# Graph network layer on one core: three buffers for gathered rows instead of five, a gather queue one turn ahead, and the statistics of the early rows moved into the turns

## The reference, cut to what matters

```python
h = relu(layernorm(x))                       # 6250 nodes x 128, float32
W = silu(edge_attr @ fw1 + fb1) @ fw2 + fb2  # 206250 edges x 50 -> x 128, the filters
t = silu(h @ aw1 + ab1) @ aw2 + ab2          # the node table
msg = W * t[src]                             # one gathered row of t for each edge
agg = segment_sum(msg, dst)                  # dst is sorted
return x + h + silu(agg @ ow1 + ob1) @ ow2 + ob2
```

## Time and profile before

| | |
|---|---|
| median of three runs | 2394.53 us (2394.49 to 2397.1) |
| the profiled execution | 2395.59 us |
| its span, first to last instruction | 2393.7 us |
| POOL busy | 1525.4 us, 64% |
| PE busy | 1300.2 us, 54% |
| DVE busy | 1178.2 us, 49% |
| ACT busy | 520.4 us, 22% |
| mean granted clock of PE | 0.74 |

### The profile page before, as it was taken

The page is one execution under the profiler, slowest core; times in us unless marked ns, Lnnn a source line. Parts: engine busy times, 40 slices in busy tenths (PEclk is TensorE's granted clock), DMA queues, the critical chain, the costliest instruction groups (busy, mean ns, idle before and its releaser), DMA issues.

```text
span 2393.7 us, 13107 instructions
## 1 busy us (share of the span) xinstructions
PE 1300.2 (54%) x4526; PEld 701.8 (29%) x4526; DVE 1178.2 (49%) x1404; ACT 520.4 (22%) x545; POOL 1525.4 (64%) x1619
## 2 busy tenths in 40 slices
PE   2425665656554655566556555655655454555545
PEld 1313332323332333233223222323332232232323
DVE  3635454545554554555535544644454453554545
ACT  2312222212221222222222211211222121121211
POOL 7246666666666666666666666666666666666664
PEclk8667776778777677777668777876778686776776
DMA  4312122212212222212212212212212212212211
GB/s 140 143 30 79 45 80 81 75 54 84 82 51 81 53 75 79 81 47 82 86 45 83 80 46 88 79 50 84 83 51 80 81 50 81 80 51 85 56 46 37
DMA packets 62292, 171.46 MB, mean 72 GB/s; under 512 B 27088, under 2 KB 29648, under 8 KB 59024
## 3 DMA queue, kind: packets, MB, share of 16 engines
q0 software_dynamic: 51584, 105.75, 17.1%
q1 hardware_dynamic: 8192, 61.32, 6.8%
q10 hardware_dynamic: 2448, 3.54, 0.4%
HBM read 164.08 MB, written 6.42 MB: 71 GB/s over the span
## 4 chain that ended last, share of the span: by engine, by line
another core or an unknown queue 40%; PE 27%; ACT 15%; issue 14%; DVE 3%; DMA 0%; ACTq 0%; SPq 0%; DVEq 0%
PE banks L872 15%; ACT hid L435 7%; PE banks L864 7%; ACT hid L441 7%; PE banks L879 3%; PE banks L887 1%; PE banks L811 1%; ACT hs L455 1%; DVE stats L643 0%; ACT mid L464 0%; DVE stats L544 0%; PE banks L806 0%; PE banks L818 0%; DMA xs<-in_x 0%
## 5 line engine op out<-in xcount | busy, mean ns | idle before, releaser
L369 POOL DMA_INDIRECT xg<-node_table,src x1564 | 1478.6, 945 | 828.3 <-issue 453.2
L872 PE MATMUL banks<-hid,wts 128*128 128x512 f32 x806 | 535.3, 799 | 565.4 <-ACT hid L435 436.6
L672 DVE TENSOR_TENSOR banks<-banks,xg 128x1024 f32<-128x1024 f32 (+1 forms) x198 | 241.0, 1217 | 1090.2 <-remote 899.2
L864 PE MATMUL banks<-attr,wts 50*128 50x512 f32 x806 | 293.9, 810 | 444.8 <-issue 250.4
L675 DVE TENSOR_REDUCE sums<-banks 128x128 f32<-128x1024 f32 (+1 forms) x408 | 493.9, 1211 | 13.6
L441 ACT ACTIVATE hid<-banks,cols 128x1024 f32<-128x1024 f32 x202 | 224.5, 1111 | 914.0 <-remote 425.7
L435 ACT ACTIVATE hid<-banks,cols 128x1024 f32<-128x1024 f32 x202 | 224.4, 1111 | 825.0 <-remote 595.9
L872 PEld LDWEIGHTS banks<-hid,wts 128*128 128x128 f32 x806 | 179.9, 248 | 755.3 <-ACT hid L435 467.6
L879 PEld LDWEIGHTS banks<-ident,hid 128*128 128x128 f32 x1612 | 225.5, 171 | 204.2 <-issue 198.2
L879 PE MATMUL banks<-ident,hid 128*128 128x128 f32 x1612 | 284.5, 333 | 0.0
L679 DVE TENSOR_TENSOR banks<-banks,other 128x1024 f32<-128x1024 f32 (+1 forms) x204 | 248.7, 1219 | 7.0
(11 more groups left out here) (89 smaller groups left out, 279.5 us busy)
## 6 DMA issues: line engine op xcount, KB each, us to landing
attr<-in_attr SPq DMA_DIRECT2D x25, 2048.0 KB
xg<-node_table,src POOLq DMA_INDIRECT x1564, 2.5
out<-res ACTq DMA_DIRECT2D x8, 256.0 KB
xs<-in_x SPq DMA_DIRECT2D x3, 512.0 KB, 6.0
node_table<-res SPq DMA_DIRECT2D x3, 512.0 KB, 2.8
out<-res ACTq DMA_DIRECT2D x5, 192.0 KB
spare<-in_dst SPq DMA_DIRECT2D x1, 808.0 KB
src<-in_src SPq DMA_DIRECT2D x1, 808.0 KB
```

What stands on the lines that cost most here:

```text
L369: pool.indirect_dma_start(xg[:, i % XG, j, :], None, table[:, :], bass.IndirectOffsetOnAxis(ap=src[:, s * L + j:s * L + j + 1], axis=0))\
L672: dve.tensor_tensor(to, to, rows_of, ALU.mult).then_inc(signal, 1)
L864: i = pe.matmul(hid_ps[:, GC * half:GC * half + GC], fw1_s[at, :], attr[at, cols_of], start=True, stop=True)
L872: i = pe.matmul(hid_ps[:, at], w["fw2_s"][:, :], hid[:, s % 2, at], start=True, stop=True)
```

## The change

- `XG` is 3 instead of 5, and `REACH = XG - LAG = 1`: POOL starts the gathers of turn s when the filters of turn s - 1 are done. Only the first three turns have no wait.
- The 48 early gathers are no longer issued in one go: those for the third to the sixth early turn wait for points of the node chunks (the transposes of chunk 0, the result of chunks 0, 1 and 3).
- The statistics of the early tiles are taken by DVE within turns 1 to 6 (8 `bn_stats` each), the moments in turn 7 and the scales in turn 9; ACT's square root comes in turn 8, between its silu activations. The first early task starts in turn 10 (before, in turn 0), and the early turns are 30, 50, 72, 92, 114, 136 instead of 20, 40, 64, 84, 108, 128.
- The one-hots are made for one turn at a time, with one `tensor_scalar` and one `scalar_tensor_tensor` of 128x88, in place of three operations of 128x176 every second turn. There are six buffers of one turn instead of three of two.
- The three parts of `fb2` are made only in the fallback loop.
- At the end ACT does the activation of the last output task ahead of the store of the one before it.

```diff
@@ -16,7 +16,7 @@
 PAIR_EDGES = L * P
 PAIRS = -(-N_EDGES // PAIR_EDGES)
 EDGE_TILES = PAIRS * L
-XG = 5
+XG = 3
 SETS = 4
 PART = 8
 EARLY_PAIRS = 6
@@ -34,8 +34,7 @@
 R_WINDOWS = 14
 RW = 453
 AGG = R_WINDOWS * RW
-BATCH = 2
-OH_SETS = 3
+OH_SETS = 6
 assert AGG >= STEP * (PAIRS - 1) + WIN and AGG >= LEAD + NODE_TILES * P
@@ -46,7 +45,7 @@
 assert len(GROUP_OF) == PAIRS and all(STEP * (n - 1) + WIN <= 512 for _, n in GROUPS)
-EARLY_TURNS = (20, 40, 64, 84, 108, 128)
+EARLY_TURNS = (30, 50, 72, 92, 114, 136)
 MAIN_TURNS = [s for s in range(PAIRS) if s not in EARLY_TURNS]
 MAIN_OF = {s: i for i, s in enumerate(MAIN_TURNS)}
 EARLY_OF = {s: i for i, s in enumerate(EARLY_TURNS)}
@@ -70,6 +69,8 @@
 for s in range(HALVED[0]):
     SUMS_AT.setdefault(s + LAG + (s in OPENS), []).append(s)
 assert SETS > LAG + 1
+
+REACH = XG - LAG
@@ -95,6 +96,12 @@
+STAT_TURNS = tuple(range(1, EARLY_PAIRS + 1))
+VAR_TURN, STD_TURN, SCALE_TURN, EARLY_FROM = 7, 8, 9, 10
+assert VAR_TURN > STAT_TURNS[-1]
+
+
+
 EARLY_STEPS = dict(relu=0, transposed=1, copied=2, first=3, middle=4, second=5, rows=6)
 OUT_STEPS = dict(first=0, middle=1, second=2, rows=3, stored=4)
@@ -106,7 +113,7 @@
 def tasks():
-    done, free, outs, halves = [], 0, list(range(len(OUTS) - 1)), list(range(2 * EARLY_PAIRS))
+    done, free, outs, halves = [], EARLY_FROM, list(range(len(OUTS) - 1)), list(range(2 * EARLY_PAIRS))
     for s in range(PAIRS):
         if s < free:
             continue
@@ -227,7 +234,7 @@
         xg = sb("xg", [P, XG, L, F])
         hid = sb("hid", [P, 2, PC])
         sums = sb("sums", [P, SETS + 2, 2, F])
-        onehot = sb("onehot", [P, OH_SETS, BATCH, 2, WIN])
+        onehot = sb("onehot", [P, OH_SETS, 2, WIN])
         e_x = sb("e_x", [P, EARLY_PAIRS * L, F])
@@ -353,7 +360,12 @@
             pool.wait_ge(s_pool, 3)
             pool.wait_ge(e_src_in, 16)
+
+            table_at = {2: (s_tr, 0), 3: (s_res, 0), 4: (s_res, 1), 5: (s_res, 3)}
             for t in range(EARLY_PAIRS * L):
+                if t % L == 0 and t // L in table_at:
+                    signal, c = table_at[t // L]
+                    pool.wait_ge(signal, run(c))
                 pool.indirect_dma_start(e_x[:, t, :], None, x[:, :],
                                         bass.IndirectOffsetOnAxis(ap=e_src[:, t:t + 1], axis=0)).then_inc(e_gathered[t // L], 16)
             pool.wait_ge(src_in, 16)
@@ -363,7 +375,7 @@
                 if i >= XG:
-                    pool.wait_ge(fil_done, run(s - 2))
+                    pool.wait_ge(fil_done, run(s - REACH))
                 for j in range(tiles_in(s)):
                     landed = half_gathered[2 * HALVED.index(s) + 2 * j // tiles_in(s)] if s in HALVED else gathered[i % XG]
                     pool.indirect_dma_start(xg[:, i % XG, j, :], None, table[:, :],
@@ -425,9 +437,6 @@
             act.wait_ge(s_cover, 4)
             act.activation(other[:, :], same, ACT.Identity, bias=ones[:, 0:1], scale=-1.0).then_inc(s_other, 1)
-            act.wait_ge(s_var, 3)
-            act.activation(e_moments[:, 2, :], e_moments[:, 2, :], ACT.Sqrt).then_inc(s_std, 1)
-
             def silu_hid(s):
                 n = tiles_in(s) * P
@@ -445,11 +454,16 @@
                     if a < PAIRS:
                         silu_hid(a)
                         add_fb2(a)
+                if s == STD_TURN:
+                    act.wait_ge(s_var, 3)
+                    act.activation(e_moments[:, 2, :], e_moments[:, 2, :], ACT.Sqrt).then_inc(s_std, 1)
             def task(kind, step, b, n):
                 if step == "relu":
                     if n >= 2:
                         act.wait_ge(n_tr, n - 1)
+                    if n == 0:
+                        act.wait_ge(s_rstd, 3)
                     for j in range(TPG):
                         t = n * TPG + j
                         i = act.activation(hs[:, n % 2, j, :], e_x[:, t, :], ACT.Relu, bias=e_moments[:, 3, t:t + 1],
@@ -471,12 +485,11 @@
             act.wait_ge(s_hx, run(N_CHUNKS - 1))
             act.wait_ge(s_left, 1)
-            act.wait_ge(s_rstd, 3)
             turns(pair, task)
+            task("out", "middle", len(TASKS), len(OUTS) - 1)
             for left in STEPS.get(PAIRS, ()):
                 task(*left)
-            for step in ("middle", "stored"):
-                task("out", step, len(TASKS), len(OUTS) - 1)
+            task("out", "stored", len(TASKS), len(OUTS) - 1)
             n = edges_left(act)
             for i in range(2):
                 act.wait_ge(s_out[i], 16 * len(OUTS[i::2]))
@@ -595,21 +608,6 @@
             i.then_inc(s_cover, 1)
             dve.tensor_tensor(low, first_ps, d_last.rearrange(flat), ALU.min).then_inc(s_cover, 1)
             dve.tensor_tensor(high, first_ps, d_last.rearrange(flat), ALU.max).then_inc(s_cover, 1)
-
-            dve.tensor_copy(fb2_part[:, 0, :], rows[:, 0, :]).then_inc(s_fb2, 1)
-            dve.wait_ge(s_fb2, 1)
-            dve.tensor_tensor(fb2_rest[:, 0, :], rows[:, 0, :], fb2_part[:, 0, :], ALU.subtract).then_inc(s_fb2, 1)
-            dve.wait_ge(s_fb2, 2)
-            dve.tensor_copy(fb2_part[:, 1, :], fb2_rest[:, 0, :]).then_inc(s_fb2, 1)
-            dve.wait_ge(s_fb2, 3)
-            dve.tensor_tensor(fb2_rest[:, 1, :], fb2_rest[:, 0, :], fb2_part[:, 1, :], ALU.subtract).then_inc(s_fb2, 1)
-            dve.wait_ge(s_fb2, 4)
-            dve.tensor_copy(fb2_part[:, 2, :], fb2_rest[:, 1, :]).then_inc(s_fb2, 1)
-            dve.wait_ge(s_fb2, 5)
-            dve.wait_ge(s_set, 1)
-            for i in range(3):
-                dve.tensor_copy(fb2_rows[32 * i:32 * i + 1, :, :],
-                                fb2_part[32 * i:32 * i + 1, i:i + 1, :].to_broadcast([1, TPG, F])).then_inc(s_fb2, 1)
             dve.tensor_tensor(ends[:, 0, :], first_ps, bases[:, :], ALU.subtract).then_inc(s_rel, 1)
             dve.tensor_tensor(ends[:, 1, :], last_ps, bases[:, :], ALU.subtract).then_inc(s_rel, 1)
@@ -637,15 +635,13 @@
             dve.tensor_scalar(n_left[:, :], left_ps, -1.0, float((EDGE_TILES + PAIRS) * P), ALU.mult,
                               ALU.add).then_inc(s_left, 1)
-            for t in range(EARLY_PAIRS * L):
-                if t % L == 0:
-                    dve.wait_ge(e_gathered[t // L], 16 * L)
-                i = dve.bn_stats(stats[:, t, :], e_x[:, t, :])
-            i.then_inc(s_step, 1)
-            step[0] += 1
-            dve.wait_ge(s_step, step[0])
-            moments_of(stats[:, 0:EARLY_PAIRS * L, :], e_moments)
-            scales_of(e_moments, 3)
+            def early_stats(r):
+                dve.wait_ge(e_gathered[r], 16 * L)
+                for t in range(r * L, (r + 1) * L):
+                    i = dve.bn_stats(stats[:, t, :], e_x[:, t, :])
+                if r == EARLY_PAIRS - 1:
+                    i.then_inc(s_step, 1)
+                    step[0] += 1
             dve.wait_ge(s_hx, run(N_CHUNKS - 1))
             dve.wait_ge(s_pool, 3)
@@ -654,15 +650,12 @@
             dve.wait_ge(s_tab, 16 * (AHEAD + table_writes(N_CHUNKS - 1)))
-            def one_hots(k):
-                first, n = k * BATCH, min(BATCH, PAIRS - k * BATCH)
-                nodes = iota[:, 0:WIN].rearrange("p (o w) -> p o w", o=1).to_broadcast([P, n, WIN])
-                for m in range(2):
-                    of_row = ends[:, m, first:first + n].rearrange("p (n o) -> p n o", o=1).to_broadcast([P, n, WIN])
-                    dve.tensor_tensor(onehot[:, k % OH_SETS, 0:n, m, :], nodes, of_row, ALU.is_equal).then_inc(oh_done, 1)
-                dve.wait_ge(oh_done, 3 * k + 2)
-                dve.tensor_tensor(onehot[:, k % OH_SETS, 0:n, 1, :], onehot[:, k % OH_SETS, 0:n, 1, :], onehot[:, k % OH_SETS, 0:n, 0, :],
-                                  ALU.subtract).then_inc(oh_done, 1)
+            def one_hots(s):
+                nodes, to = iota[:, 0:WIN], onehot[:, s % OH_SETS, :, :]
+                dve.tensor_scalar(to[:, 0, :], nodes, ends[:, 0, s:s + 1], None, ALU.is_equal).then_inc(oh_done, 1)
+                dve.wait_ge(oh_done, 2 * s + 1)
+                dve.scalar_tensor_tensor(out=to[:, 1, :], in0=nodes, scalar=ends[:, 1, s:s + 1], in1=to[:, 0, :],
+                                         op0=ALU.is_equal, op1=ALU.subtract).then_inc(oh_done, 1)
             def by_tile(s, h, n):
@@ -687,8 +680,7 @@
             def pair(s):
-                if s % BATCH == 0:
-                    one_hots(s // BATCH)
+                one_hots(s)
                 if s in HALVED:
                     by_halves(s)
                     return
@@ -711,6 +703,13 @@
                 mask(msg, s * L, L, masked)
                 dve.wait_ge(masked, run(s))
                 row_sums(s % SETS, 1, msg).then_inc(red_done, 1)
+                if s in STAT_TURNS:
+                    early_stats(STAT_TURNS.index(s))
+                elif s == VAR_TURN:
+                    dve.wait_ge(s_step, step[0])
+                    moments_of(stats[:, 0:EARLY_PAIRS * L, :], e_moments)
```

(20 more changed lines are left out.)

## The result

The kernel took 2356.81 us in the median of four runs (2353.55 to 2362.83), against 2394.51 for the one before beside it. The ratio is 0.9846, with a 95% interval of 0.9822 to 0.9869: 37.7 us off, where I had forecast 17.5. The profiled execution took 2358.69 us, with a span of 2356.9.

The account below looks back on a forecast made before the run. The prediction took PE's signals, arriving late when POOL has issued gathers for long, to bound the kernel. Terms -20 + 2 + 3 + 3 - 6 = -18 gave a span of 2375.7, hence 2377 us, range 2332 to 2436.

Parts of the forecast that it names:

- places and reach: Steady turns: no price; the loop through DVE's sums asks 6.2 us a turn, hidden under POOL's 10.0.
- +2 (statistics): Turns 1 to 6: 1.9 us of DVE statistics in each, of which the first flush may show one, +2 us.
- +3 (root): Early turns: the root takes ACT out of its silu tables and back, +3 us, between 0 and 18.
- +3 (one-hots): All turns: the new one-hot operations touch POOL's gathers, taken as +3 us; DVE's own time 0.
- The start: Up to turn 5's gathers: first main gather at 90, turn 3 at 140, turn 5 at about 164, -20 us.
- this wait goes: Start: PE's hidden no longer waits until ACT has the root at 155.78; part of the start's -20 us.
- The end: After the last gathers begin: the last multiply follows about 8 us later, before 15.4; -6 us (0 to -9).
- A stop each turn: Rival, steady turns: filters arrive over 10.0 us after the last, so every turn stops; +300, 2677 us, chance 0.08.
- Long stretches go: Rival, steady turns: POOL's three-turn stretches break into twos, some 16 more stops of 3.4; +55, 2432 us, chance 0.20.
- The compare locks POOL: Rival, one-hots: the new tensor_scalar compare holds up POOL's gathers, +34 instead of +3; 2408 us, chance 0.05.
- Start gains nothing: Rival, start: held signals move from the early gathers to the first 24 main ones; +20, 2397 us, chance 0.10.
- Sooner signals: Rival: stops come after less running, half are 2 us shorter, the start gains more; -40 more, 2337 us, chance 0.12.

## Why the prediction was too small

**What bounds the kernel: right, with a limit that I didn't see.** Late signals bound it, and they went on doing so as forecast (waits after the first 305.6 us, forecast 305). I took them for a property of kernel and chip. They are a condition that comes and goes, and a saving that consists of shorter late signals goes with it. And I laid them on PE, while DVE's own steps come late as well. In the loop of places and reach four operations of 1.23 are 4.9 us and not 5.1, which changes nothing.

**The step that failed is the middle,** the terms +2 (statistics), +3 (root), +3 (one-hots), and no price for places and reach. It measured -3.4 instead of +8: 11.4 of the missing 18.9 us; the start and the end, each sized too small, make the other 4.7 and 2.8. None of the three +'s shows in POOL's times. All the 48 statistics are done by 188, behind the sums of turns 1 to 6, at 9.8 us against 11.2 with 11.9 of gaps before. The root with its two loads of tables:

```profile
201.64 1.28 ACT L459 ACT_TABLE_LOAD   x1
202.94 0.24 ACT L459 ACTIVATE e_moments<-e_moments 128x48 f32<-128x48 f32 x1
203.20 1.28 ACT L444 ACT_TABLE_LOAD   x1
...
213.34 1.11 ACT L450 ACTIVATE hid<-banks,cols 128x1024 f32<-128x1024 f32 x1 [7.73 <-issue]
```

It takes ACT 2.8 us. PE's `hidden` for the next silu ended at 202.81, so that silu comes some 1.6 us later than it could. Behind it PE ends the filters' product at 209.34 and ACT takes it at 213.34, 4.0 us late, so the 1.6 were probably swallowed. The kernel with all of this ahead of the turns isn't fit to price it with late signals: its middle of 2186.0 is of another batch, and its ratio, 0.9837, differs from 0.9846 by less than the intervals. Without late signals the two middles were level (1904.4 and 1905.6).

The one-hots: gathers took 1479.0 us instead of 1478.6. The Trainium skill (SBUF — State Buffer, section "Who interferes with whom") has `tensor_scalar` as an operation that may lock GpSimd out; 202 of them at 273 ns beside gathers of 946 ns against 945 show no such lock of the gathers here: the 195 gathers that had a compare beside them took 947 ns, the others 945. By that rule the term would have been near the +34 of the rival. It was the old `tensor_tensor` compares that cost a little, 966 ns for the 111 gathers beside them against 944, 2.4 us in all. In the other direction a lock isn't ruled out: a new compare takes 255 ns in the median and up to 485.

**Places and reach do have a price, a negative one.** Three places alone take 18 us off the kernel before (12 to 24 by the interval). Of that the end is 27.8 - 19.7 = 8.1, the start gives 3.1 back, and about 13 must lie in the middle. This is what is left of the ratio, and no trace shows it: the two middles are 2199.8 and 2182.0, the wrong way round, from batches that lie 18 us apart. In the changed kernel, five places against three are 0.9898 against 0.9846, from two batches whose intervals just touch: 12 us, of which the end is 6.6. Within a batch there are two pairs of single executions, which differ in more than the places: a middle of 2177.6 (three places, gathers in one go) against 2195.4 (the turns of before), and 2186.0 (three, statistics first) against 2205.8 (five). They support the sign; the size is not shown. The number of stops doesn't explain the middle: 83 pauses before, 83 with three places, 85 after, 80 after with five. Their mean is 3.6 us after against 4.1 with five places, but 3.9 in the kernel before with three against 3.7 without; one execution of each can't tell. Why three places shorten the middle stays open.

**The start: right in sign, near in size, and with the shares of its causes wrong.** Forecast were 90 for the first main gather, 140 for turn 3, 164 for turn 5; 95.66, 136.36 and 159.31 came, the first too late and the other two earlier than forecast, so two errors cancel in part. Beside the earlier table I laid the gain on the wait for the root (155.78), "this wait goes". (It was ACT's silu that waited, behind the root in ACT's order; PE's `hidden` had run at 114.90.) With five places the steps can be added up: 183.96, held-back gathers 171.12 (-12.8), and with the statistics and the small operations moved too 158.95 (-12.2). Three places change little at that point (159.31). But with three places the statistics are worth only 163.63 - 159.31 = 4.3, though the first silus are 11.1 apart (108.68 and 119.74). For POOL stops after three turns in both, at 125.5 and 123.5, and in the changed kernel the bias of turn 1 is held for that stop (126.09, 12.4 us after that of turn 0), so most of its lead is lost. As I read it, two cures for the same wait don't add up. The held-back gathers do, by 166.10 - 159.31 = 6.8, though the median of that run doesn't resolve it. Their own line, in the kernel before with nothing else changed:

```profile
91.99 0.94 POOL L373 DMA_INDIRECT xg<-node_table,src  x1 [9.71 <-DMA node_table<-res]
...
140.91 0.24 ACT L433 ACTIVATE e_moments<-e_moments 128x48 f32<-128x48 f32 x1 [43.37 <-DVE e_moments L516]
...
171.12 0.94 POOL L373 DMA_INDIRECT xg<-node_table,src  x1 [29.48 <-PE banks L883]
```

The root no longer waits for the end of POOL's five turns: it comes at 140.91, while they end at 141.6 (before: 155.78 and 152.3). In both kernels DVE's six steps up to it come every 1.4 us beside the gathers. The gathers began 10.7 us earlier, the statistics too (104.07 instead of 114.76), and all behind them came earlier.

**The end: right mechanism, -8.8 instead of -6.** It is the ring's: 25.6 with five places in the changed kernel, 17.6 to 19.7 with three. Without late signals it isn't there (16.6 with five and with three). I had the last multiply 8 us after the last gathers began; it was 2344.75 - 2337.87 = 6.9.

**The rivals.** "A stop each turn" was mis-thought, not only unlikely: even with no reach there are 92 pauses for 196 turns. "Long stretches go" didn't happen (85 pauses against 83). "The compare locks POOL" is out. "Start gains nothing" is out with late signals; without them turn 5 even begins 3.8 us later than before (118.14 against 114.33), for the stop at turn 3 and not for the rival's reason. "Sooner signals" with its 2337 is 20 us off, like the forecast's own 2377; its mechanism is not shown.

**No version beats both kernels in both conditions by what was run.** With late signals the changed kernel is the fastest (with statistics first, or with the early gathers in one go, it is level); without, five places are, which with late signals still take 1.0% off. Four places are level with five without late signals, 0.9976, and were not run with them.

## What to carry to other kernels

Before pricing a change, ask what condition the bound itself depends on, and run the kernel before again on its own: here one and the same kernel took 2034 or 2410 us, and the change was worth 1.5% or nothing. Where two edits cure the same wait, price the second with the first in place. And a queue that never pauses can cost more than one that stops: holding POOL's early gathers back until the table had got further took 12 us off the kernel before (8 to 20 by the interval of the ratio), without moving any work off an engine.

## What the hardware showed that I had not expected

- The late signals come and go: with the same program, the same 945 ns for a gather and the same 1211 ns for a sum on DVE, spans were 2393.7 and 2032.0 us. The time of the DMA packets of the gathers is nearly the same too (17.1% of 2393.7 us and 19.5% of 2032.0). PE's mean granted clock was 0.74 and 0.78; whether this is a cause or follows from PE's longer waits is not told apart, but a slower PE doesn't delay what it has already ended. What else differs between the batches is not in the traces.
- They don't only hit what PE signals: DVE's statistics, which wait for nothing that the profile shows, got gaps of 0.2 to 1.8 us after POOL had gathered for 17.6 us, and steps that follow one another on DVE came every 1.4 us instead of every 0.26.
- They nearly go where POOL issues gathers with pauses: with four for eight, ACT's nameless waits for PE fell from 1049.0 to 41.1 us. Small memsets between the gathers don't help, so it is not the kind of the instruction alone; whether it is the issue or its traffic is not told apart.
- An instruction of 116 ns on POOL between two gathers of a turn is free, as it lies in the 0.30 us that follow each (1.251 us from gather to gather with it, 1.252 without).
- Half the gathers took the kernel to 1339 us: under POOL's 10.0 us a turn the other engines need some 6.
